# A two-layer graph network: the smallest edge kind multiplied from gathered rows in place of its node tables

## The reference

```python
h = relu(layernorm(x))
feat = concat([h[src], h[dst]], axis=1)              # 8192 x 2048
e_hh = relu(feat[:256] @ W_hh + b_hh)                # W_*: 2048 x 1024
e_oo = relu(feat[256:1536] @ W_oo + b_oo)
e_ho = relu(feat[1536:] @ W_ho + b_ho)
logit = concat([e_hh, e_oo, e_ho]) @ W_a + b_a       # one number per edge
alpha = softmax of logit over the edges with the same dst
z = segment_sum(alpha * h[src], dst)
x = x + relu([h | z] @ W)          # W_hn for the first 128 nodes, W_on for the rest
# layer 1: h2 = relu(layernorm(x)), x + D^-1/2 (A + I) D^-1/2 (h2 @ W1.T + b1)
```

## Time and profile before

| what | value |
|---|---|
| median of 3 runs | 657.75 us (657.56 to 659.94) |
| the profiled execution | 657.6 us |
| its span in the trace | 655.6 us |
| PE, DVE, ACT, POOL busy | 86%, 73%, 44%, 27% |
| moved by DMA | 140.5 MB, mean 214 GB/s |

### The profile page before, as it was taken

One profiled execution on the slowest core, in us unless ns is written; L12 is line 12 of the kernel. 1 busy time (PEld: TensorE's weight loads), 2 busy tenths in 40 slices (PEclk: granted clock), 3 DMA queues, 4 the chain that ended last, 5 costly groups with the idle time before them and its releaser, 6 DMA issues.

```text
span 655.6 us, 8151 instructions
## 1 busy us (share of the span) xinstructions
PE 561.7 (86%) x2373; PEld 415.1 (63%) x2377; DVE 477.3 (73%) x934; ACT 287.5 (44%) x466; POOL 176.7 (27%) x164
## 2 busy tenths in 40 slices
PE   0799999999859996979898997567949999869987
PEld 0688777776626774656575764333738878657866
DVE  6715266776998999989989996486796289783252
ACT  2622321113076555556655465489852183322200
POOL 2000200265464754565536553300030000000000
PEclk9999999999879998989898998788978899969999
DMA  8444553499999999999999998853456066121021
GB/s 315 140 137 151 184 189 109 149 277 382 304 299 349 308 317 303 349 314 337 299 350 304 289 349 285 191 178 113 130 178 239 16 227 196 60 82 47 0 81 48
DMA packets 55973, 140.51 MB, mean 214 GB/s; under 512 B 6274, under 2 KB 6402, under 8 KB 55938
## 3 DMA queue, kind: packets, MB, share of 16 engines
q0 software_dynamic: 20624, 74.98, 37.6%
q1 hardware_dynamic: 27072, 50.34, 22.7%
q10 hardware_dynamic: 8242, 14.75, 6.0%
HBM read 123.27 MB, written 16.78 MB: 214 GB/s over the span
## 4 chain that ended last, share of the span: by engine, by line
PE 40%; DVE 30%; DMA 15%; issue 7%; ACT 4%; POOL 3%; ACTq 0%; DVEq 0%; POOLq 0%
PE ps L615 22%; DMA gath<-tab_b,tabl_i 10%; DVE gath L870 6%; PE ps L601 6%; DVE ring_l L845 4%; DVE gath L865 4%; PE ps L774 3%; DMA tab_b<-stage 3%; DVE onehot L887 2%; PE ps L746 2%; PE ps L565 2%; ACT onehot L474 2%; PE ps L759 2%; DMA gath<-tab_a,tabl_i 2%; POOL gath L287 2%
## 5 line engine op out<-in xcount | busy, mean ns | idle before, releaser
L615 PE MATMUL ps<-ring_h,actT_h 128*128 128x512 f32 x520 | 228.2, 439 | 25.7 <-ACT stage L445 9.1
L615 PE MATMUL ps<-ring_h,actT_l 128*128 128x512 f32 x520 | 208.6, 401 | 0.0
L615 PE MATMUL ps<-ring_l,actT_h 128*128 128x512 f32 x520 | 207.7, 400 | 0.0
L474 ACT ACTIVATE onehot<-onehot,lgs 128x512 bf16<-128x512 bf16 x192 | 124.6, 711 | 96.3 <-DVE onehot L887 87.8
L427 ACT CAST ring_h<-raw 128x512 fp32r<-128x512 f32 x176 | 104.8, 617 | 117.5 <-PE ps L615 86.3
L845 DVE TENSOR_TENSOR ring_l<-raw,ring_h 128x512 fp32r<-128x512 f32 x176 | 116.8, 685 | 31.9 <-ACT ring_h L427 31.4
L615 PEld LDWEIGHTS ps<-ring_h,actT_h 128*128 128x128 f32 x520 | 101.0, 194 | 60.5 <-ACT stage L445 12.0
L615 PEld LDWEIGHTS ps<-ring_h,actT_l 128*128 128x128 f32 x520 | 100.6, 194 | 23.0
L287 POOL DMA_INDIRECT gath<-tab_a,tabl_i x64 | 73.0, 1141 | 156.3 <-DVE gath L870 71.7
L615 PEld LDWEIGHTS ps<-ring_l,actT_h 128*128 128x128 f32 x520 | 101.4, 195 | 20.7
L565 PE MATMUL ps<-onehot 128*128 128x512 bf16 x290 | 83.9, 398 | 23.7 <-ACT onehot L474 19.7
(11 more groups left out here) (157 smaller groups left out, 488.9 us busy)
## 6 DMA issues: line engine op xcount, KB each, us to landing
raw<-in_L_gnn_W_ho_dram SPq DMA_DIRECT2D x32, 256.0 KB
raw<-in_L_gnn_W_oo_dram SPq DMA_DIRECT2D x32, 256.0 KB
raw<-in_L_gnn_W_hh_dram SPq DMA_DIRECT2D x32, 256.0 KB
raw<-in_L_gnn_W_on_dram SPq DMA_DIRECT2D x32, 256.0 KB
raw<-in_L_gnn_W_hn_dram SPq DMA_DIRECT2D x32, 256.0 KB
tab_a<-stage ACTq DMA_DIRECT2D x24, 256.0 KB
tab_b<-stage ACTq DMA_DIRECT2D x24, 256.0 KB
raw<-in_L_gnn_W_dram SPq DMA_DIRECT2D x16, 256.0 KB
```

The costliest lines, as they stand in the source:

```text
L474: ins = nc.scalar.mul(onehot[:, s, 1 + i, :], onehot[:, s, 1, :], lgs[:, i, q:q + 1])
L615: mm = nc.tensor.matmul(ps[:, first + m, :], w, v, start=(k == 0 and i == 0), stop=(k == KT - 1 and i == 2))
```

## The change

The kind hh has only 256 edges, fewer than the 512 nodes. Its tables go, and its edge rows are multiplied directly:

- SP stores h to h_d (behind the loads of chunk 0), ACT loads the hh edges' nodes as columns (hh_i), and POOL gathers 4 tiles of h rows (src and dst of 2 tiles) into gath slots 4 to 7.
- In chunk 0, before k = 5 and k = 7, TensorE transposes them (32 transposes); ACT and DVE make featT_h and featT_l (hh_high, hh_low). featT_h lies over hrow, which SP reloads from h_d after chunk 7.
- Order of kinds: ho (chunks 0 to 3), hh (4 to 7), oo (8 to 11). The hh chunks have 2 tiles of edges in place of 4 of nodes, 6 matmuls a step, and one group of banks runs over both halves. DVE adds the bias and does relu, times W_a and row sum out of the banks (hh_edges): no store, no gather.
- Counting begins in chunk 1: 16 tiles a chunk in 1 to 3, the last 16 in chunks 4 and 5.
- Sums: hh first, in chunk 8; 7 tiles each in 9 to 11, 16 in chunk 12, 7 in 13, 8 in 14, 7 in 15, and three (LAST_SUMS) behind it. Edges: 10 in chunks 5 to 7, 8 in each of 8 to 12, 9 in 13 and 14, the last three behind chunk 15. copy_a and copy_b come at k = 0 of the next chunk also where they came at k = 2.

```diff
+            load_chunk(W_ho, 0, 0, 0)
+            for m in range(NM):
+                sp.wait_ge(s_h, m + 1)
+                sp.dma_start(h_d[m * P:(m + 1) * P, :], hrow[:, m, :]).then_inc(s_hd, 16)
...
+            chunk_done(sp, CH_HH + 3)
+            sp.wait_ge(s_hd, 16 * NM)
+            for m in range(NM):
+                sp.dma_start(hrow[:, m, :], h_d[m * P:(m + 1) * P, :]).then_inc(s_hrow, 16)
...
+            pool.wait_ge(s_hidx, 64)
+            pool.wait_ge(s_hd, 16 * NM)
+            for i in range(2 * T_HH):
+                pool.indirect_dma_start(out=gath[:, NM + i, :], out_offset=None, in_=h_d[:, :],
+                                        in_offset=bass.IndirectOffsetOnAxis(ap=hh_i[:, i:i + 1], axis=0)).then_inc(s_hg[i], 16)
...
-            for q in range(FIRST, ET):
-                if q in (T_HO, T_HO + T_OO):
-                    tables_landed(kinds_of(q))
+            for q in range(FIRST, TG):
+                if q == T_HO:
+                    tables_landed(2)
...
+            for e, end in enumerate((src, dst)):
+                for t in range(T_HH):
+                    act.dma_start(hh_i[:, 2 * t + e:2 * t + e + 1], end[t * P:(t + 1) * P].rearrange("(p a) -> p a", a=1)).then_inc(s_hidx, 16)
...
+            def hh_transposes(k):
+
+                if k in (5, 7):
+                    if k == 5:
+                        pe.wait_ge(s_spanok, 1)
+                        for i in range(2 * T_HH):
+                            pe.wait_ge(s_hg[i], 16)
+                    for b in range(NM):
+                        j = b + (0 if k == 5 else NM)
+                        if k == 7:
+                            pe.wait_ge(s_ftl, b + 1)
+                        for f in (2 * j, 2 * j + 1):
+                            for t in range(T_HH):
+                                c = f % 2 * E_HH + t * P
+                                mm = nc.tensor.transpose(ps[:, b, c:c + P], gath[:, NM + 2 * t + f // KT, f % KT * P:(f % KT + 1) * P], ident[:, :])
+                        mm.then_inc(s_ftp, 1)
+
+            def hh_chunk(n, half):
+
+                q = CH_HH + 2 * n + half
+                for k in range(KT):
+                    pe.wait_ge(s_low, RAW + q * KT + k + 1)
+                    f = half * KT + k
+                    for t in range(T_HH):
+                        b = NM + 2 * n + t
+                        if half == 0 and k == 0:
+                            pe.wait_ge(s_copied, 4 * NM + 2 * n + t + 1)
+                        for i, (w, v) in enumerate(passes(featT_h[:, f, t * P:(t + 1) * P], featT_l[:, f, t * P:(t + 1) * P],
+                                                          ring_h[:, k, :], ring_l[:, k, :])):
+                            mm = nc.tensor.matmul(ps[:, b, :], w, v, start=(f == 0 and i == 0), stop=(f == 2 * KT - 1 and i == 2))
...
+                    mm.then_inc(s_slot, 1)
+                    later_counts(q, k)
...
+            def hh_edges(n):
+
+                dve.wait_ge(s_bias, 48)
+                for t in range(T_HH):
...
+                    step(nc.vector.tensor_tensor(ps[:, b, :], ps[:, b, :], bias2[:, 0, c], ALU.add))
+                    nc.vector.scalar_tensor_tensor(out=ps[:, b, :], in0=ps[:, b, :], scalar=0.0, in1=wa_b[:, c],
+                                                   op0=ALU.max, op1=ALU.mult, accum_out=lgh[:, t, n:n + 1]).then_inc(s_hhd, 1)
...
+        EDGE_AT = {(5, 1): 0, (5, 5): 1, (6, 0): 2, (6, 2): 3, (6, 4): 4, (6, 6): 5, (7, 0): 6, (7, 2): 7, (7, 4): 8, (7, 6): 9}
+        EDGE_AT |= {(8 + i, k): 10 + i * KT + k for i in range(5) for k in range(KT)}
...
+            INVERSE_AT = {(5, 7): (2, 0), (6, 3): (2, 1), (6, 7): (2, 2), (7, 3): (2, 3)}
+            INVERSE_AT |= dict(zip([(c, k) for c in range(8, 12) for k in (3, 6)], [(t, k) for t in range(2) for k in range(NM)]))
...
+            for p in LAST_EDGES:
+                edge(p)
+            split_logits(LAST_EDGES[0], TG)
+            for p in LAST_SUMS:
+                logit_onehots(p)
+            copy_kind(1)
```

More of the change, by code:

```diff
@@ L120, in gnn_kernel @@
         assert at["end"] <= nc.sbuf_usable_end
+        featT_h = sb("featT_h", [P, 2 * KT, E_HH], F32R, over="hrow")
+        featT_l = sb("featT_l", [P, 2 * KT, E_HH], F32R, over="logit_d")
         hrow_h = sb("hrow_h", [P, NM, D], F32R, over="gath")
@@ L158, in gnn_kernel @@
         s_h = sem("h_rows")
+        s_hd = sem("h_stored")
+        s_hrow = sem("h_reloaded")
+        s_hidx = sem("hh_edges_loaded")
+        s_hg = [sem(f"hh_rows_gathered{i}") for i in range(2 * T_HH)]
+        s_ftp = sem("hh_transposed_banks")
+        s_fth = sem("hh_transposed_high")
+        s_ftl = sem("hh_transposed_low")
+        s_hhc = sem("hh_banks_done")
+        s_hhd = sem("hh_banks_read")
         s_norm = sem("h_normed")
@@ L210, in gnn_kernel @@
         PLAIN = [q for q in range(T_HO + T_OO) if q % 2]
-        USES = [(q, e) for q in range(ET) for e in ((0, 1) if q in PLAIN else (0,))]
+        USES = [(q, e) for q in range(TG) for e in ((0, 1) if q in PLAIN else (0,))]
         USE = {u: c for c, u in enumerate(USES)}
-        ADDED = {q: sum(1 for p in range(q + 1) if p not in PLAIN and USE[p, 0] % GB == USE[q, 0] % GB) for q in range(ET)}
+        ADDED = {q: sum(1 for p in range(q + 1) if p not in PLAIN and USE[p, 0] % GB == USE[q, 0] % GB) for q in range(TG)}
         TP_H = KT
@@ L334, in _ @@
                     gather_add(q - LAG, kinds_of(q - LAG))
[L335 to L336 removed]
+            for q in range(TG - LAG, TG):
+                if q not in PLAIN:
+                    gather_add(q, 2)
             pool.wait_ge(s_ohu, OS + 2 * ET)
             for i in range(4):
[L340 removed]
+                pool.wait_ge(s_st[i], 16 * (len(TABLES) + 2))
             bias(0, b_hn)
@@ L621, in chunk, with edge_chunk @@
                         after(k)
-            def edge_chunk(q, before=None, after=None):
-                chunk(q, NM, range(NM), lambda m: pe.wait_ge(s_copied, q * NM + m + 1), before, after, counted=True)
+            def edge_chunk(q, i, before=None, after=None):
+                chunk(q, NM, range(NM), lambda m: pe.wait_ge(s_copied, i * NM + m + 1), before, after, counted=True)
             reg = [None]
@@ L692, in _, with sums @@
-            edge_chunk(LAST_COUNTS, after=last_counts)
-            pe.wait_ge(s_ccopy, 3)
-            open_masked(0)
-            with pe.Fori(0, 6) as i:
-                edge_chunk(i + 6, before=lambda k: uniform_sums(i, k))
+                if k:
+                    add_logits(i * TC + k - 1, k - 1, k % OS, 2 + i * TC + k - 1)
+            def sums(tiles):
+                for q in tiles:
+                    if q == TG:
+                        open_masked(2, 1)
+                    if q == T_HO:
+                        pe.wait_ge(s_kfree, 2 * NM)
+                        open_masked(1, 3)
+                    if q % TC == 0 or q in (21, T_HO, TG):
+                        reg[0] = codes(q // TC, TC)
+                    add_logits(q, q % TC, SLOT[q], ORDER[q])
+                    if q in KIND_ENDS:
+                        close_banks(s_kind)
@@ new lines, in _ @@
+            edge_chunk(0, 0, before=hh_transposes)
+            pe.wait_ge(s_ftl, KT)
+            open_banks()
+            with pe.Fori(0, LOOP_COUNTS) as c:
+                edge_chunk(c + FIRST_COUNTS, c + FIRST_COUNTS, after=lambda k: count_tiles(c * 2, k))
+            reg[0] = codes(48 // G, G)
+            for n in range(NN):
+                for half in range(2):
+                    hh_chunk(n, half)
+            pe.wait_ge(s_hhd, 2 * T_HH)
+            pe.wait_ge(s_ccopy, 3)
+            edge_chunk(CH_OO, 4, before=lambda k: sums(SUMS_AT.get((CH_OO, k), ())))
@@ L697, in _ @@
+            pe.wait_ge(s_kfree, NM)
+            open_masked(0, 2)
+            with pe.Fori(0, 3) as i:
+                edge_chunk(i + CH_OO + 1, i + 5, before=lambda k: uniform_sums(i, k))
             q = CH_EDGE
-            base = NM + NM * CH_EDGE
-            waits = (NM * CH_EDGE + 1, None, base + 4, None)
+            base = NM + NM * len(TABLES)
+            waits = (base - NM + 1, None, base + 4, None)
             for c, (_, _, _, ms) in enumerate(NODE[0]):
@@ L704, in _ @@
                     free = lambda m: pe.wait_ge(s_copied, waits[c] + (m if c == 0 else 0))
-                chunk(q + c, NM, ms, free, before=lambda k: last_sums(q + c, k))
+                chunk(q + c, NM, ms, free, before=lambda k: sums(SUMS_AT.get((q + c, k), ())))
+            sums(LAST_SUMS)
             pe.wait_ge(s_kfree, 3 * NM)
```

293 lines of the change are left out of this document (158 added, 135 removed).

## The result

The changed kernel took 665.2 us at the median of its runs (664.7 to 668.8), the kernel before 658.6 beside it: a ratio of 1.011, 95% interval 1.007 to 1.015. It is slower by 1.1%; 642.0 was forecast, 630 to 650 as its own range (chance 0.65) and 623 to 656 as the wider one.

The account below looks back on a forecast made before the run. TensorE alone bounds up to 122.6 us, then DMA, VectorE and TensorE are nearly full. Bounds on T of 457 (VectorE), 455 (DMA), 450 (pace) gave 454: 657.6 - (467.2 - 454) - 2.4 = 642.0, range 630 to 650.

Parts of the forecast that it names:

- The beginning: Up to chunk 3's end: new transposes, earlier counting and index transposes add 9.9 us, so it ends at 132.5, not 122.6.
- The rival of the late gathers: Chunk 0: early gathers land after 39.7 instead of 33, TensorE stands and each us costs one; chance 0.03.
- Chunks 4 to 7: The short chunks run at VectorE's pace, 66.1 us of its work, not TensorE's 44 + 10.
- The clock's rival: Chunks 4 to 7: TensorE waits, its clock falls, the stretch takes 108 us at 1.2 GHz, time 684; chance 0.06.
- The pace behind it: After the first ten tiles, done at 198.6, 52 tiles at 4.6 us each reach 437.8; T = 449.9 by this bound.
- VectorE's sum: From chunk 3's end to T: 289.4 us busy plus 34.8 idle after 132.5, giving T = 456.7.
- The rest, 34.8, I keep: VectorE's idle time up to T, 47.0 us before less 12.2, stays: late gathers, a kind's banks, the last chain.
- The term of 12.2: VectorE's 5.61 + 6.63 us idle behind the smallest kind's tables before T, held by tables_landed(3) on POOL, goes.
- The tail: From the last gather's landing at 440.8 to T: 14.5 us for the last tiles, giving T = 455.3 by DMA.
- After T: T is the last copy_kind's end, taken as 454; behind it 2.4 us of low halves go, leaving 186 us.
- The later start not made good: Tile work starts 9.9 us later and DMA gives 310 GB/s: T = 463.1, time 651 to 657; chance 0.14.
- One price of a rival: VectorE's floor, gathers in time up to T: only 9 us idle, T = 431, time 619, half way 628; chance 0.12.

Follow-up runs that it names:

- Experiment 1: Two of three multiplications of one-hots by logit parts left out for 41 tiles: changed kernel 0.9949, kernel before 0.9908, as ratios to the kernel before.
- Experiment 3: Changed kernel with its sums dealt otherwise over chunks 9 to 15, in three ways, nothing left out: 1.0071, 1.0039 and 1.0030 of the kernel before.
- experiment 8: Cuts of work together: changed kernel with ACT and DMA cuts 0.9762, with VectorE's too 0.9633; kernel before with all three 0.9601.
- experiments 2, 3 and 5: Changed kernel reordered: last edges earlier 1.0031; sums dealt otherwise 1.0071, 1.0039, 1.0030; the last of these with thirteen tiles in chunks 5 to 7, 1.0119.
- a_start: Changed kernel with 8 of the 32 new transposes in chunk 0: 1.0061 of the kernel before.

## Why the prediction was wrong, step by step

**The beginning: right.** Forecast +9.9, chunk 3 to end at 132.5; it ends at 133.1. The first gather from tab_b is issued at 136.8 (137.3). The parts were less good than their sum: the 32 transposes take 3.9 us and not 5.2, while the early gathers land much later than 33. The chain there:

```profile
17.27 7.08 DMA h_d<-hrow
...
25.16 1.04 POOL gath L315
...
30.01 9.75 DMA gath<-h_d,hh_i
39.76 0.14 issue
39.90 1.94 PE ps L731 x16
```

The 6 us of cover were used up: landed at 39.76, wanted at 39.3, TensorE waits 0.6 us. The rival of the late gathers was nearer than its 0.03 said. The stretch from 30 to 39.8 shows why: with the loads of the weights beside them the DMA engines are full.

```profile
30.00:39.80 9.80, 9.28 (x41) 7.34 (x40) 4.68 (x13) 2.29 (x4) 0.94 (x1) 1.00 1.01 383
```

**Chunks 4 to 7: mis-sized.** 66.1 us by VectorE's work, 73.2 measured. VectorE is busy 62.7 in them and waits 10.5, of which the longest is 6.5 us for the copy of a count of edges by ACT (count_d), whose place in the lists moved into these chunks; it was not priced at all. The work itself was priced 3.4 too high. VectorE's longest waits there:

```profile
DVE logit_d L1028 <- ACT count_d L485: 6.5, 1, 6.5
DVE ring_l L956 <- ACT ring_h L480: 2.8, 1, 2.8
```

From 127.4 to 200 the DMA engines were full in the kernel before, at a share of 1.00 and 310 GB/s; now it is 0.85 and 269. Ten tiles were done by then in the forecast at 198.6; the tenth's edge comes at 205.1. The clock's rival (a mean of 0.66 needed) stayed out: the granted clock was 0.88.

**The pace behind it: right.** 4.6 us a tile forecast; from tile 9 to tile 58 it is 230.1 / 49 = 4.70 (5 us more over the 49 tiles), with the DMA engines at 324 GB/s in chunks 8 to 11 (318 forecast). The DMA share leaves 1.0 near 437 to 440, the last gather being issued at 432.3; the queue of the gathers moves its last bytes between 441 and 442 (landing forecast at 440.8). The Trainium skill ("DMA: Bandwidth & Descriptors", Specifications) gives about 358 GB/s as one core's limit, half of what a memory stack gives. The trace of this kernel, which runs on one core, is above it in a short stretch, 383 from 30 to 39.8; over the stream of tiles it stays below, at 324, and that is the figure that goes with the pace measured.

**VectorE's sum: the work right, the idle time wrong.** Busy 289.4 forecast, 288.2 measured. The step "The rest, 34.8, I keep" failed by 20.6 us: 10.5 in chunks 4 to 7 (13.6 before), 14.6 in chunks 8 to 11 (6.4 before), 30.3 from chunk 12 on (27.1 before, or 14.9 without the 12.2). Of the 14.6, 11.6 are waits for gathers (4.7 before).

The term of 12.2 was also misread. The hold of tables_landed(3) on POOL is gone, and with it the wait on the third kind's store, but only 6.63 of the 12.2 stood behind it. POOL in the kernel before:

```profile
392.83 2.48 POOL L301 DMA_INDIRECT gath<-tab_b,tabl_i  x1 [0.30 <-issue]
...
408.40 1.53 POOL L287 DMA_INDIRECT gath<-tab_a,tabl_i  x1 [9.95 <-issue]
```

The gather that VectorE awaited for 5.61 us, until 404.36, is the one issued at 392.83, before the hold began; it took 11.5 us. Waits of this sort stayed: VectorE still stands 7.8 us for gathers from 350.8 on.

**The tail: the step that decided.** "Only the tail is then left: ... 14.5." From the forecast landing, 440.8, to T are 35.8 us: 21.3 more, of the 22.6 by which T missed its forecast (476.6 for 454). The forecast counted the last three tiles alone, on engines that stand ready. But ACT had 19 more tiles' parts in its list from chunk 12 on, 35.6 us, and the last edges stood behind chunk 15's low halves. ACT was 44% busy over the span and so appears in none of the three bounds (VectorE, DMA, pace); the order of the sums, written in the diff, says how many tiles are left for the last chunks. That the tail is this long is measured; that ACT's list alone makes it so is not. Experiment 1 shows that leaving out part of ACT's work gives the changed kernel 1.6% and the old one 0.9%. Experiment 3 shows that moving the sums earlier delays the gathers and exposes TensorE's list, at a T only a few us earlier.

**After T: right.** 186 forecast, 186.1 measured.

**The rivals.** The later start not made good (651 to 657) had the right mechanism and was still too cheap: the stage doesn't run at any one engine's rate. The forecast took a value among three bounds, each reckoned on one engine as if the others stood ready; experiment 8 shows that the delays of three engines add, within its intervals. One price of a rival was off in its own terms: half way between 619 and 642 is 630.5, not 628. What stays open: how the 1.1 us of gain left in the stage divides into the 44 us of TensorE's products saved and the losses just named. Experiment 3 thins out the late chunks for ACT, but no run does it for every engine with all work left in. A better order of the same work may exist; of the five tried (experiments 2, 3 and 5) none did better than the kernel before.

## What to carry to other kernels

When work leaves one engine and the stream that feeds the end starts later, count for every engine, also one that is 44% busy, what its list holds in the last chunks, before and after: what could no longer be done early is done there. Where several engines are each 80 to 90% full and run written-out lists, the largest of their bounds was too low a forecast here; idle time seen before is not a constant, and a removed wait's us are to be had only if no other list is late by less. And a relief that is worth a fifth to a half of its size on each of three engines is a sign of such a stage: cut two at once and see whether the gains add.

## What the runs showed of the hardware

- In the 9.8 us from 30 to 39.8, in which the four gathers of h rows run beside loads of weights, the profile has 383 GB/s at a DMA share of 1.01, against 317 to 324 in the long stretches of the stream of tiles at a share of 1.00. The share alone doesn't tell what the engines move. The last gather landed 9.75 us after its issue, where 5.1 had been taken from x's loads.
- h's store to memory (4 x 512 KB) took 6.6 us at the median, x's loads of that size 5.2.
- TensorE's clock fell to 0.67 in a_start after a stretch with 2.1 us of idle time in 8.3, and took the 1.5 us won by fewer transposes back.
